# One half of a running sum added by accumulating DMA transfers instead of GpSimd instructions

## The reference

```python
def step(h, ins):
    dt_t, u_t, B_t, C_t = ins
    h = jnp.exp(dt_t[..., None] * A) * h + (dt_t * u_t)[..., None] * B_t[:, None, :]
    y_t = jnp.einsum('bdn,bn->bd', h, C_t)
    return (h, y_t)
_, ys = jax.lax.scan(step, h0, xs)
y = jnp.moveaxis(ys, 0, 1) + u * Dp
y = y * jax.nn.silu(z)
return jnp.einsum('bld,ed->ble', y, Wout)
```

## Time and profile before

| | |
|---|---|
| median of 3 runs | 6933.95 us (6899.48 to 6969.27) |
| profiled execution | 6937.52 us, its span 6935.8 us |
| mean granted clock of PE | 0.803 |
| busy: PE, DVE, ACT, POOL | 76%, 68%, 60%, 71% |
| DMA queue of SP | 302.80 MB, 13.6% of 16 engines |

### The profile page before, as it was taken

The page is one execution under the profiler, slowest core; times in us unless marked ns, Lnnn a source line. Parts: engine busy times, 40 slices in busy tenths (PEclk is TensorE's granted clock), DMA queues, the critical chain, the costliest instruction groups (busy, mean ns, idle before and its releaser), DMA issues.

```text
span 6935.8 us, 82733 instructions
## 1 busy us (share of the span) xinstructions
PE 5245.0 (76%) x21900; PEld 3287.9 (47%) x21900; DVE 4746.4 (68%) x6116; ACT 4128.6 (60%) x6696; POOL 4905.2 (71%) x3914
## 2 busy tenths in 40 slices
PE   3786877878777777877878777777877878787665
PEld 2344454444545445454444545444454544545444
DVE  3258577675867767587676867767586776767774
ACT  1366565665666566566666656566566666656563
POOL 0177777777777777677777777777777777777784
PEclk6678788787888878788788888878788887878777
DMA  3011111011111111111111111111111111111110
GB/s 107 25 33 45 42 50 48 30 55 36 45 52 48 45 33 44 44 50 48 38 53 38 45 44 49 45 33 56 36 47 50 45 48 34 43 44 46 36 47 25
DMA packets 152792, 308.76 MB, mean 45 GB/s; under 512 B 20870, under 2 KB 58310, under 8 KB 149926
## 3 DMA queue, kind: packets, MB, share of 16 engines
q1 hardware_dynamic: 152278, 302.80, 13.6%
HBM read 285.90 MB, written 16.84 MB: 44 GB/s over the span
## 4 chain that ended last, share of the span: by engine, by line
PE 41%; issue 19%; POOL 18%; DVE 10%; ACT 9%; DMA 2%; POOLq 0%; SPq 0%; DVEq 0%; ACTq 0%
PE psum L1303 9%; POOL arena_m L719 9%; PE psum L1493 8%; POOL arena_m L730 5%; PE psum L1347 3%; PE psum L1473 3%; PE psum L1426 3%; PE psum L1363 2%; DVE arena_m L1160 2%; PE psum L1418 2%; PE psum L1318 2%; DVE arena_m L1210 2%; POOL arena_a L677 2%; PE psum L1448 1%; PE psum L1435 1%
## 5 line engine op out<-in xcount | busy, mean ns | idle before, releaser
L719 POOL TENSOR_TENSOR arena_m<-bS,arena_m 128x512 f32<-128x512 f32 x2048 | 2599.3, 1285 | 183.2 <-PE psum L1493 155.3
L1210 DVE TENSOR_TENSOR_SCAN arena_m<-psum,arena_m 128x512 f32<-128x512 f32 x2048 | 2448.4, 1210 | 345.4 <-ACT psum L939 170.2
L1493 PE MATMUL psum<-ident,arena_m 128*128 128x128 f32 x8192 | 1524.6, 323 | 661.3 <-DVE arena_m L1221 285.3
L730 POOL TENSOR_TENSOR arena_m<-arena_m,hc 128x512 f32<-128x512 f32 x1024 | 1307.3, 1277 | 1009.6 <-ACT hc L947 829.4
L1493 PEld LDWEIGHTS psum<-ident,arena_m 128*128 128x128 f32 x8192 | 1166.0, 167 | 1413.7 <-issue 738.4
L939 ACT ACTIVATE psum<-arena_m,Aneg 128x512 f32<-128x512 f32 x2048 | 1397.6, 689 | 389.9 <-DVE arena_m L1210 375.3
L1221 DVE SCALAR_TENSOR_TENSOR arena_m<-psum,Ct,arena_m 128x512 f32<-128x512 f32 x1024 | 750.5, 733 | 512.4 <-PE psum L1493 511.0
L1303 PE MATMUL psum<-arena_a 64*128 64x512 f32 (+3 forms) x2048 | 895.3, 568 | 227.9 <-DVE arena_m L1176 127.1
L947 ACT ACTIVATE hc<-psum,Ct 128x512 f32<-128x512 f32 x1024 | 693.9, 678 | 362.9 <-PE psum L1493 278.7
L811 ACT ACTIVATE arena_a<-psum 128x384 f32<-128x384 f32 (+1 forms) x768 | 400.8, 524 | 547.2 <-PE psum L1303 546.6
L1303 PEld LDWEIGHTS psum<-arena_a 64*128 64x128 f32 x2048 | 411.8, 230 | 589.7 <-issue 288.1
(11 more groups left out here) (151 smaller groups left out, 7374.3 us busy)
## 6 DMA issues: line engine op xcount, KB each, us to landing
bS<-brow SPq DMA_DIRECT2D x512, 256.0 KB, 3.3
wB<-kept_B SPq DMA_DIRECT2D x16, 1408.0 KB, 6.2
wU<-kept_U SPq DMA_DIRECT2D x32, 512.0 KB, 4.1
wZ<-kept_Z SPq DMA_DIRECT2D x32, 512.0 KB, 5.1
wO<-kept_O SPq DMA_DIRECT2D x32, 512.0 KB, 4.5
wA<-kept_A SPq DMA_DIRECT2D x16, 768.0 KB, 6.8
wB<-kept_B SPq DMA_DIRECT2D x16, 768.0 KB, 4.3
wA<-kept_A SPq DMA_DIRECT2D x16, 640.0 KB, 4.8
```

The source lines that it names most:

```text
L719: pool.tensor_tensor(hb[s % HBS][:, m, :], bS[:, s % 2, :], du[r][:, m, :], ALU.mult).then_inc(m_dbu.sem, 1)
L730: pool.tensor_tensor(yT[:, 2 + i, :], yT[:, 2 + i, :], hc[:, i, :], ALU.add).then_inc(m_yl.sem, 1)
L1210: dve.tensor_tensor_scan(v, EB[j % EBS], v, 0.0, ALU.mult, ALU.add).then_inc(m_scan.sem, 1)
L1493: ins = pe.transpose(HT[pos % 2][:, m * P:(m + 1) * P], hb[s % HBS][:, m, i * P:(i + 1) * P], ident[:, :])
```

## The change

`add_last` no longer computes: GpSimd issues a DMA transfer whose source is `hc[:, i, :]` and whose destination is `yT[:, 2 + i, :]`, with an add on arrival, 256 KB in SBUF on either side. The counter `m_yl` becomes two, one for each `i`, counted by 16 for each transfer. The three places that waited for the POOL add (the next add of the same `i`, `weigh_last`, `turn_back`) wait for the transfer to have landed. `apart` is a bare semaphore increment between two waits.

```diff
-        m_y, m_hc, m_yl = signal("m_y", SLOTS // 2), signal("m_hc", SLOTS // 2), signal("m_yl", SLOTS // 2)
+        m_y, m_hc = signal("m_y", SLOTS // 2), signal("m_hc", SLOTS // 2)
+        m_yl = [signal(f"m_yl{i}", 16 * SLOTS // NT) for i in range(2)]
...
                 if n == 0:
                     pool.wait_ge(*m_y0.by(b, NT * r + 2 + i + 1))
                 else:
-                    pool.wait_ge(*m_yl.by(b, c - 1))
-                pool.tensor_tensor(yT[:, 2 + i, :], yT[:, 2 + i, :], hc[:, i, :], ALU.add).then_inc(m_yl.sem, 1)
+                    pool.wait_ge(*m_yl[i].by(b, 16 * s))
+                apart(pool)
+                pool.dma_start(yT[:, 2 + i, :], hc[:, i, :], accum_op=ALU.add).then_inc(m_yl[i].sem, 16)
...
                 act.wait_ge(*m_hT.by(b, NT * s + 2 * i + 2))
-                act.wait_ge(*m_yl.by(b, c - 1))
+                act.wait_ge(*m_yl[i].by(b, 16 * s))
                 act.activation(hc[:, i, :], HT[1], ACT.Copy, scale=Ct[:, r, 2 + i, n:n + 1]).then_inc(m_hc.sem, 1)
...
                 if i < 2:
                     pe.wait_ge(*m_y.by(b, 2 * (NS * (r + 1) - 1) + i + 1))
                 else:
-                    pe.wait_ge(*m_yl.by(b, 2 * (NS * (r + 1) - 1) + i - 1))
+                    pe.wait_ge(*m_yl[i - 2].by(b, 16 * NS * (r + 1)))
```

## The result

The changed kernel takes 7196.23 us (median of 3 runs, 7185.86 to 7224.35) against 6933.95: a ratio of 1.0385, 95% interval 1.0345 to 1.0425, 262 us slower. The forecast was 7082 us with a range of 6850 to 7450.

What follows compares the result with a forecast made beforehand. No engine is full; PE holds 41% of the chain, POOL 18%, the add 340 us. 6937.5 + 19 (issue on POOL) + 90 + 39 (later sum) = 7085.5 us profiled, stated as 7082 us, range 6850 to 7450.

Steps and rivals of the forecast that it cites:

- What bounds the kernel: Whole kernel: no engine is full, PE holds 41% of the chain, POOL 18%; removing the add brings at most 340 us.
- The POOL term, +19 us: On POOL: an issue takes 1.34 us against 1.27 for an add, on the 268 adds on the chain: +19 us.
- the prediction's own rule: On POOL: the term is 268, the adds on the chain, times issue time less the add's 1.27 us.
- wrong, faster: Sign in the profile after: products of `inflow` in POOL's gapless stretch follow each other with less than 0.8 us between.
- The rival of the cheap issue: POOL issues in 0.32 us, term -255 us, kernel 6742 us; an issue below 0.79 us decides the sign; chance 0.17.
- the rival at the 1.0 us of the Trainium skill: POOL's software issue takes 1.0 us: -72 us there, delays stay at +129, kernel 6994 us; chance 0.12.
- The landing: 4.1 us taken: Behind POOL: priced like SP's 512 KB transfers, the sum is ready 2.8 us later than by an add (1.7 to 5.7).
- +90 and +39 us: Delays from the later sum: +90 us at the mid-sequence turn (`weigh_last`, `d_turn`), +39 us for ACT's other `hc` waits.
- The rival "absorbed": An issue costs what the add did and slack takes up the delays at the turn: 6937 us, no change; chance 0.14.
- The cover of the next transfer: On POOL: the same block's next transfer comes four slots later, covering a landing up to 7.4 us: no cost.
- `inflow`'s wait for `bS`: On POOL: 26.1 us in all before, with four slots of cover, so added DMA traffic was counted as nothing.
- the 12 to 24% expected: On the DMA engines: the added 268 MB, read twice over, takes some 12% to 24% more of their time.

Runs made afterwards that it cites:

- e7: The kernel before with only a semaphore increment in place of POOL's add: 6687.11 us, ratio 0.9637.
- e4: The kernel before with POOL's add over 256 of its 512 columns: 6741.93 us, ratio 0.9718.
- e3: The changed kernel with the transfer issued from ACT's queue as a plain copy, nothing in its place on POOL: 6711.46 us, ratio 0.9679.
- e9: The changed kernel with the accumulating transfer over 256 of the 512 columns: 7200.21 us, ratio 1.0391.
- e15: e5 with a third buffer for `hc`, so ACT need not wait for the transfer before last: 6934.25 us, ratio 1.0035.
- e6: The kernel before, adds kept, plus a POOL-issued transfer of 16 bytes a partition between spare buffers behind each add: 7391.49 us, ratio 1.0666.
- e8: The kernel before, adds kept, plus a spare POOL add over 256 columns ahead of each add: 7067.77 us, ratio 1.0209.
- e5: The changed kernel with POOL waiting, ahead of each product, for its own previous product: 6954.44 us, ratio 1.0046.
- e12: The kernel before with POOL waiting, ahead of each product, for its own previous product: 6902.95 us, ratio 0.9966.
- e13: e5 with a one-column POOL memset and a wait for it behind each issue: 6940.28 us, ratio 1.0022.
- e2: The changed kernel with a plain copy, still issued by POOL, in place of the accumulating transfer: 6940.39 us, ratio 1.0004.
- e14: e3 with a second transfer per sum into HBM, all who wait waiting for both: 6800.87 us, ratio 0.9827.

## Why the prediction was right, and where it was not

**What bounds the kernel: right.** POOL's 18% of the chain was worth time: without the add the kernel is 252 us faster (e7), of the 340 us that the prediction called the most that could go.

**The POOL term, +19 us: mis-sized.** It took 1.34 us for an issue, the middle between 0.32 and 2.35. Measured are 0.9 us. "So the busy time that leaves POOL as an add comes back as an issue" is wrong: POOL is busy 365 us less and its share of the chain falls by a third. By the prediction's own rule the term is 268 x (0.9 - 1.27) = -99 us, on the line of e4 about -130 us. The sign that it gave for "wrong, faster" came up, the products on either side of an issue stand 0.56 us apart in the rows, in a kernel that was slower. The rival of the cheap issue put its point of decision at 0.79 us; 0.9 us lies just above it and should have made a kernel within 1% of before. It lost 262 us, so the rule itself was incomplete. The same goes for the rival at the 1.0 us of the Trainium skill (DMA: Bandwidth & Descriptors, Latency and other measured facts): the measured cost of an issue lies next to it, its 6994 us do not lie next to the time, and no row here shows a first byte.

**The landing: 4.1 us taken, 3.3 measured.** Pricing it like a transfer of twice the bytes was 0.8 us too much. The waits came where they were said: ACT's for a free `hc`, and PE's at `d_turn`. Their price, +90 and +39 us, did not. `d_turn` lost 30 us of PE's time over the whole kernel in place of 45. A landing of 2.3 us costs 24 us or nothing (e3), 0.6 us less of it brings nothing that shows (e9), and 245 us of ACT's waits are worth 8 to 20 us (e15). The rival "absorbed" described this half correctly, but not the issue, which is cheaper than an add, and its time was wrong. Two small slips in the working change no term: two products and one add are 3.85 us by the means of the earlier trace rows, not 3.7, and the low end of ACT's waits is 70 x 1.7 / 5 = 24 us, not 18.

**What was costed at nothing.** The cover of the next transfer held: no wait of POOL for its own transfer. `inflow`'s wait for `bS` is 20.9 us (26.1 before), and the transfers take 21.9% of the DMA engines, within the 12 to 24% expected. These two were right.

**The step that failed is one that is missing.** The prediction asked who waits for POOL's data and POOL's queue, and never what POOL's instructions do to DVE, which waits for neither. Before, this already cost DVE something: its small operations took about 1.2 us beside adds and products. A DMA issue turned that into 3.3 us and more. Shown: the cost is there without bytes or landing (e6 against e8, 324 us at equal POOL time), and goes when POOL pauses for itself (e5, 235 us; control e12, 0.3%). With the measured issue of 0.9 us and landing of 3.3 us the prediction's own sum is -99 us on POOL and 2.0 / 2.8 of 129, +93 us, for the delays: within 10 us of no change. What it lacks is about the whole of the measured loss.

The sum by the runs, against before: -130 us for POOL (line of e4), +235 us for the part of DVE's standstill that e5 takes away, +24 us for the landing (e3), which makes +129 of 262. **The remaining 133 us are open.** The terms are not clean either: the line of e4 has a gain of DVE in it, so its -130 us are more than POOL's time was worth, and the landing's 24 us are within the noise. DVE in e5 is still busy 131 us longer than in e4, and e13 takes this away and pays with some POOL time; that speaks for the rest of the same standstill as a part, but e13 is still no faster than before, so it can't be shown to be all. PE's granted clock moves with the time in these runs and wasn't held apart. A standstill-free issue at no POOL cost, which would settle it, wasn't found.

So the forecast of "slower by over 1%" came true because two errors met: a term for POOL that was 150 us too high and delays priced some 100 us too high stood in for a cost of DVE that was not in the sum. In that the sign was luck. No version that computes the whole sum beats the kernel before by over 1% (e2, e3, e4, e7, e9 and e14 leave part of it out); the best is e12, the kernel before with POOL's wait, at 0.9966.

## What to carry to other kernels

Moving work from an engine to a transfer that the same engine must issue frees only the difference, here 1.23 less 0.9 us; and the issue may cost an engine that takes no part in it. Look at the small operations of VectorE in the trace, those of a few columns: if their mean rises while their number stays, read VectorE and GpSimd side by side in time. Where software-issued DMAs on GpSimd can't be avoided, a wait of GpSimd for its own previous instruction is a cheap thing to try (235 us here); better is to keep the issue on another engine where the transfer allows it (229 us between e2 and e3).

## What the runs showed of the hardware

- A DMA issued by GpSimd, with the instructions queued right behind it, holds VectorE's small SBUF operations out across instruction boundaries: 3.30 us for an operation beside others of its kind at 0.13 and 0.16 us, and a mean of 4.52 us for a cast that takes 0.67 us in e5. Without DMA issues VectorE gets in after each GpSimd instruction (1.19 us; 236 of 237 operations that stood still in the kernel before).
- An accumulating transfer of 256 KB from SBUF to SBUF costs GpSimd 0.9 us and lands in 3.3 us; the plain copy of the same bytes 0.60 us and 2.3 us. It needs 147456 packets in place of 81920 and 21.9% of the DMA engines in place of 10.3%. Half the columns don't make the issue cheaper (1.01 us mean against 1.02).
- A DMA issue on GpSimd is shown with its duration in the busy time here (1024 of POOL's 3914 instructions), and overlaps the next instruction. The distance between starts (0.6 us) is too low a price for an accumulating one, since the instruction behind it ends 0.3 us later than it would behind a plain copy; the distance between ends (0.9 us) has both.
- A one-column GpSimd memset with a wait behind the issue, beside the waits of e5, lets VectorE in at every GpSimd end (none of 112 standing operations spans one) and costs GpSimd 0.25 us.
